# A token stage rearranged: zero fill of the slot buffers in eight parts, VectorE's order in the blocks, slot assignment, and a gather ring for the last group

## The chip, the cores and the metric

One core of one Trainium2 chip runs the whole kernel. The metric is the device time of one execution in microseconds (us). Inputs and outputs live in HBM; the core's five engines are TensorE (PE, with its weight loads shown apart as PEld), VectorE (DVE), ScalarE (ACT), GpSimd (POOL) and SyncE (SP). SP does no arithmetic here: it issues nearly all direct DMAs, in a hand-written order.

## What is computed

Two sequences of L = 2048 tokens with D = 256 features in float32. First an attention block is added to x, then a mixture of experts, run in two rounds (C = 2), is added to that:

```python
x = x + attention(layernorm(x))                # 16 heads of 64, causal, latent of 64
h = layernorm(x); xf = h
for j in range(2):                             # two rounds
    gate = xf @ router_W[j] + router_b[j]
    ids = top_2(gate + gate_bias[j])           # of E = 6 experts
    weights = softmax over the two of gate
    combined = sum of weights * expert(xf)     # up 256x256, silu gate 256x256, down
    share_out = two shared experts (xf)        # for every token
    y = xf + combined + share_out
    xf = y * rsqrt(mean(y*y) + EPS) * norm_w[j]
x = x + xf
```

To come near float32 accuracy a product is made of a high part and a low part of each operand, so most matrix products take three passes. A high part is written by ScalarE, its low part is the difference that VectorE or GpSimd takes.

## The kernel before, in words

build_weights (L69) and build_attention (L210) fill the first 1945 us; nothing in them is changed. build_tokens (L900) is the rest. It works on **blocks** of 512 tokens, 4 tiles of 128 each (TPB = 4). A sequence has 4 blocks (QB = 4), so a round has 8: r = 0 to 7 is round 0, r = 8 to 15 is round 1. A **group** g is a sequence in a round (g = 0 to 3), with 16 tiles of 128 tokens (JT = 16). A **unit** u = 4r + j is a tile of 128 tokens of block r in a round.

For a block of round 0 the kernel loads the attention's partial result (load_y, L971, four copies of 512 KB, i = 0 to 3), splits it (split_y on ScalarE, y_lo_even on VectorE), projects it (project on PE, L1161), adds the residual x (residual), takes mean and variance (moments, then rstd on GpSimd) and writes the normalized tokens into xcur (layernorm). Then, for blocks of both rounds: turn transposes them; the router gives 6 logits per token (L1194); choose (L1775) finds the top two and their weights; the shared expert goes up, gated and down in four k steps (L1228; gated, L1870, multiplies the silu by the up half on VectorE, and its result starts the next pair of matmuls), add_gated sums the halves, xt_lo and g_lo make low parts, take_shared(r) (L1886) adds the shared result to the tokens of block r one block later, and SP stores it (store_acc) to a buffer in HBM, from which load_acc fetches it later.

The two experts of a token are reached through **slots**. A group's 4096 (token, expert) pairs are sorted by expert into TILES = 37 tiles of 128 rows, SLOTS = 4736 rows of 1 KB. places and slots (L1844 to L1868) work out the row of each pair in the block that ends the group (r % 8 == 3 before the change), tile_experts which expert a tile has. GpSimd scatters the tokens to x_slots with indirect DMAs (L1629), 32 per group. Rows without a pair must be zero, so both x_slots buffers are filled from a zero tile before (L1081 to L1084); the first scatter waits for this through the semaphore "cleared". Behind the 8 blocks come tiles(c), 74 **expert tiles** with a load (load_tile, L1017), three layers and a store into e_slots. In the next round GpSimd gathers each token's two rows from e_slots (gather, L1640, into a ring of 4 buffers), and VectorE adds them with their weights (add_first and add_second, L1955 and L1962), takes variance; GpSimd makes the root (rms), VectorE normalizes. For units 16 to 31 (blocks 4 to 7) this lies in blocks 9 to 12: group 1's second half of round 0 is turned into the inputs of blocks 12 to 15 there. Units 48 to 63 (blocks 12 to 15, group 3) are done in a **tail** behind tiles(1), and so are the shared experts of blocks 14 and 15 (LATE).

Orders written out by hand: SP's queue (L1059 to L1147), and block_of of each engine: PE L1299, ACT L1490, POOL L1650, DVE L1987. An engine works strictly in its order. In VectorE's block_of before the change, a block of round 1 opened with eight adds of gathered rows and variance(r-5), then choose(r); a block of round 0 with moments(r+1) and choose(r), then layernorm(r+1) and two y_lo_even, and gated(r, 0) only behind these. In r = 3 and r = 11 places, slots and tile_experts closed the block. At the very end SP clears every semaphore of the stage one by one (clear_semaphores, L61), 99 of them.

## Time and profile before

| | us |
|---|---|
| median of 3 runs (lowest to highest) | 3025.83 (3025.55 to 3028.52) |
| the profiled execution: own time | 3039.41 |
| the profiled execution: span in the profile | 3037.7 |
| PE busy in the span | 2717.7 (89%) |
| DVE busy | 1923.0 (63%) |
| POOL busy | 1946.6 (64%) |
| ACT busy | 1721.3 (57%) |

The profile is of one execution; its own time is 13.6 us above the median of the runs. Times in a row are us from the start of the span unless marked ns. L12 is line 12 of the kernel before. A row of the timeline reads: start, duration, engine, line, operation, output<-inputs, shape, count of instructions put together, and in brackets how long the engine stood before it and for what. Tiles bear the name of the memory they lie in: the zero tile appears as accr, the ring of gathered rows and the raw y loads as yg, a loaded expert tile as work.

### The profile page before, as it was taken

What the parts mean: (1) busy time and instruction counts of PE and PEld (TensorE: products, weight loads), DVE (VectorE), ACT (ScalarE), POOL (GpSimd) and SP (SyncE); (2) the same over time, 40 slices, a digit from 0 to 9 for tenths busy, and PEclk for the clock granted to TensorE, in tenths of its full rate; (3) what the DMA queues carried; (4) which work ended last, traced back from release to release, by engine and by line L of the source; (5) the groups of instructions that cost most, each with busy time, mean ns of one, the idle gap of its engine ahead of it and who ended that gap; (6) DMA issues with size and microseconds to landing.
All of it is one profiled execution on the core that took longest, in us unless ns stands there. A gap on an engine that the chain in (4) does not pass through costs nothing. (4 is left out here: it accounts for less than half of the span.)

```text
span 3037.7 us, 57326 instructions
## 1 busy us (share of the span) xinstructions
PE 2717.7 (89%) x13656; PEld 2252.5 (74%) x13656; DVE 1923.0 (63%) x4379; ACT 1721.3 (57%) x4016; POOL 1946.6 (64%) x1743
## 2 busy tenths in 40 slices
PE   5899999999998599999999999689889997579993
PEld 4688778878886378787778788578777886468872
DVE  3777777777783677777777776245544463544555
ACT  2477777777777277777777778433223452214442
POOL 2588889888897289888898888522342232343234
PEclk9799999999999699999999999889989998779996
DMA  3001001000011101110010001373333441124452
GB/s 67 10 23 28 22 21 25 22 21 23 19 26 23 37 17 22 23 25 19 25 25 22 19 22 22 92 251 118 111 111 125 141 140 57 54 90 141 154 178 91
DMA packets 165661, 186.93 MB, mean 62 GB/s; under 512 B 56957, under 2 KB 130947, under 8 KB 165385
## 3 DMA queue, kind: packets, MB, share of 16 engines
q1 hardware_dynamic: 152072, 150.17, 16.8%
q0 software_dynamic: 12288, 33.57, 3.4%
q14 instruction: 196, 1.60, 0.3%
q8 instruction: 81, 1.33, 0.2%
q10 hardware_dynamic: 1024, 0.26, 0.0%
HBM read 100.56 MB, written 78.64 MB: 59 GB/s over the span
## 5 line engine op out<-in xcount | busy, mean ns | idle before, releaser
L363 POOL TENSOR_TENSOR pl<-pr,ph 128x512 fp32r<-128x512 f32 (+3 forms) x1184 | 1375.3, 1186 | 199.5 <-ACT ph L612 171.4
L609 ACT ACTIVATE pr<-ps 128x512 f32<-128x512 f32 (+3 forms) x1280 | 692.1, 541 | 430.4 <-DVE ps L737 192.0
L786 DVE TENSOR_REDUCE part<-ps 128x1 f32<-128x512 f32 (+3 forms) x1152 | 705.6, 618 | 142.8 <-PE ps L446 123.0
L612 ACT ACTIVATE ph<-ps 128x512 fp32r<-128x512 f32 (+3 forms) x1280 | 692.1, 541 | 0.0
L446 PE MATMUL ps<-k_hi,q_parts 128*128 128x512 f32 (+3 forms) x1280 | 496.2, 390 | 48.2 <-DVE part L786 23.5
L460 PE MATMUL ps<-q_parts,k_hi 128*128 128x512 f32 (+3 forms) x1280 | 488.1, 381 | 0.3
L480 PE MATMUL ps<-ph,v_hi 128*128 128x512 f32 (+3 forms) x1280 | 476.8, 372 | 8.1 <-POOL pl L363 8.0
L461 PE MATMUL ps<-q_row,k_lo 65*128 65x512 f32 (+3 forms) x1280 | 474.2, 370 | 0.0
L481 PE MATMUL ps<-ph,v_lo 128*128 128x512 f32 (+3 forms) x1280 | 470.0, 367 | 0.0
L482 PE MATMUL ps<-pl,v_hi 128*128 128x512 f32 (+3 forms) x1280 | 467.3, 365 | 0.0
L446 PEld LDWEIGHTS ps<-k_hi,q_parts 128*128 128x128 f32 x1280 | 247.7, 194 | 135.5 <-DVE part L786 59.2
L1228 PE MATMUL ps<-xt,share_up 128*128 128x512 f32 x768 | 228.2, 460 | 74.3 <-DVE work L1879 67.3
L480 PEld LDWEIGHTS ps<-ph,v_hi 128*128 128x128 f32 x1280 | 244.9, 191 | 62.9 <-POOL pl L363 17.3
L460 PEld LDWEIGHTS ps<-q_parts,k_hi 128*128 128x128 f32 x1280 | 243.8, 190 | 60.7 <-ACT ph L612 10.8
L481 PEld LDWEIGHTS ps<-ph,v_lo 128*128 128x128 f32 x1280 | 245.0, 191 | 38.1
L482 PEld LDWEIGHTS ps<-pl,v_hi 128*128 128x128 f32 x1280 | 242.8, 190 | 39.6
L461 PEld LDWEIGHTS ps<-q_row,k_lo 65*128 65x128 f32 x1280 | 244.7, 191 | 32.1
L1228 PEld LDWEIGHTS ps<-xt,share_up 128*128 128x128 f32 x768 | 169.6, 226 | 120.9 <-DVE work L1879 72.1
L737 DVE TENSOR_TENSOR ps<-ps,mask_kq 128x128 f32<-128x128 f32 x512 | 149.9, 293 | 154.2 <-PE ps L461 121.7
L1640 POOL DMA_INDIRECT yg<-e_slots,slot_i x128 | 125.1, 977 | 176.0 <-PE ps L1349 106.8
L1349 PE MATMUL ps<-exp_up,yy 128*128 x888 | 234.8, 400 | 0.0
L675 POOL TENSOR_TENSOR q_parts<-q_raw,q_parts 64x512 fp32r<-64x512 f32 x128 | 175.0, 1367 | 79.5 <-DVE q_parts L731 61.9
(203 smaller groups left out, 3830.1 us busy)
## 6 DMA issues: line engine op xcount, KB each, us to landing
work<-x_slots SPq DMA_DIRECT2D x148, 128.0 KB
e_slots<-work SPq DMA_DIRECT2D x148, 128.0 KB
rec<-recip_rows SPq DMA_DIRECT2D x128, 128.0 KB, 3.4
y_latent<-y_sums SPq DMA_DIRECT2D x128, 128.0 KB, 2.9
yg<-y_latent SPq DMA_DIRECT2D x32, 512.0 KB
x_slots<-accr SPq DMA_DIRECT2D x2, 4736.0 KB, 23.7
acc_shared<-accw SPq DMA_DIRECT2D x14, 512.0 KB
accr<-acc_shared SPq DMA_DIRECT2D x14, 512.0 KB
```

The lines of the kernel that those rows point to most:

```text
L363: eng.tensor_tensor(pl[:, s % RING, 0:w], pr[:, s % RING, 0:w], f32(ph[:, s % RING, 0:w]), ALU.subtract).then_inc(sem, 1)
L446: pe.matmul(ps[:, MAX_BANK + m % 2, 0:w], qa[half][:, i * P:(i + 1) * P], kh[:, c * BLK:c * BLK + w], start=True, stop=True).then_inc(S["m ...
L460: pe.matmul(out, kh[:, k], qa[half][:, q], start=True, stop=False)
L461: pe.matmul(out, kl[0:LD + 1, k], qc[half][:, q], start=False, stop=True).then_inc(S["scored"], 1)
L480: pe.matmul(out, va[:, kt, :], ph[:, b, 0:w], start=kt == 0, stop=False)
L481: pe.matmul(out, vc[:, kt, :], ph[:, b, 0:w], start=False, stop=False)
L482: pe.matmul(out, va[:, kt, :], pl[:, b, 0:w], start=False, stop=kt == TPB * (qb + 1) - 1).then_inc(S["latent_used"], 1)
L609: act.activation(pr[:, s % RING, 0:w], src, ACT.Exp).then_inc(S["probs"], 1)
L612: act.activation(ph[:, s % RING, 0:w], src, ACT.Exp).then_inc(S["probs_hi"], 1)
L786: ins = dve.tensor_reduce(dst, src[:, 0:w], AX.X, ALU.max)
L1228: mm = pe.matmul(out, sup[:, a, kind, n, dt, m * P:(m + 1) * P], xt[:, x, dt, :], start=i == 0, stop=i == len(terms) - 1)
L1349: mm = pe.matmul(out, tx[:, t % 2, x, dt, :], wu[:, b, bass.ds(expert[t], 1), dt, :], start=False, stop=n == len(terms) - 1)
```

## The change

- **Zero fill.** Instead of two copies of 4736 rows each ahead of the blocks, SP issues one part of 1184 rows (1.16 MB) in each of blocks 0 to 7, behind the block's loads and ahead of store_acc(r-1): 74 partitions write 16 rows of 1 KB each. Parts 0 to 3 fill buffer 0 (semaphore cleared0), 4 to 7 buffer 1 (cleared1); the first scatter of group 0 and of group 1 each wait for their own.
- **Start-up.** y loads 2 and 3 of block 0 are issued right behind x of block 0, ahead of the weights. ScalarE splits the router's weights behind all of split_y(0), VectorE its low part behind layernorm(0); PE makes the shared weights (make_shared) before turn(0, 0).
- **VectorE's order in a block.** choose, gated 0, weigh, gated 1, layernorm(r+1), normalize(r-6), (in r % 8 == 4) places and slots of the group before, y_lo_even, gated 2 and 3, xt_lo, take_shared, add_gated, then tile_experts, the adds of gathered rows and variance, the rest of y_lo_even, and moments(r+2) last. split_down is halved over blocks 6 and 7. ScalarE's squares follow its block work, and rms and normalize of a block of group 1 come one block later than before (10 <= r < 14).
- **Tail.** Group 3's gathers go to 16 buffers of their own (late, in the memory of the experts' up weights wu), each with its own semaphore, so they wait for no add. The low parts g_lo of blocks 14 and 15 move from GpSimd to VectorE (late_lo). The order of adds, take_shared(14) and normalize is rearranged, and two silus of block 15 go ahead of four squares.
- Semaphores of the stage: 17 more (cleared becomes two, 16 late).

Indentation is shortened in the diff:

```diff
...
   with ExitStack() as ctx:
-    names = ["small_in", "stage0", "stage1", "filled", "zeroed", "cleared",
+    names = ["small_in", "stage0", "stage1", "filled", "zeroed", "cleared0", "cleared1",
...
          "gathered0", "gathered1", "gathered2", "gathered3",
+         *[f"late{n}" for n in range(JT)],
...
     eo = wk[:, 8 * D:12 * D].rearrange("p (k d) -> p k d", d=D)
+    late = f32(W["wu"][:, :, :, :, :]).rearrange("p a e t i -> p (a e t i)")[:, 0:2 * JT * D].rearrange("p (u k d) -> p u k d", k=2, d=D)
...
-        load_y(0, 0)
-        load_y(0, 1)
+        for i in range(2):
+          load_y(0, i)
         load_x(0)
+        for i in range(2, 4):
+          load_y(0, i)
...
                  w["router_w"][c].rearrange("(t p) e -> p t e", p=P)).then_inc(S["small_in"], DMA)
-        load_y(0, 2)
-        load_y(0, 3)
...
         load_y(2, 1)
-        sp.wait_ge(S["zeroed"], 1)
-        for b in range(2):
-          sp.dma_start(x_slots[b].rearrange("(t p) d -> p t d", p=P),
-                 F["zero"][:, None, :].broadcast_to([P, TILES, D])).then_inc(S["cleared"], DMA)
...
             load_expert(2 * r + 3)
+          if r == 0:
+            sp.wait_ge(S["zeroed"], 1)
+          sp.dma_start(x_slots[r // QB].rearrange("(a p k) d -> a p k d", a=QB, k=16)[r % QB],
+                 F["zero"][0:SLOTS // 64, None, :].broadcast_to([SLOTS // 64, 16, D])).then_inc(S[f"cleared{r // QB}"], DMA)
...
         project(0)
+        make_shared()
         turn(0, 0)
-        make_shared()
...
-        def split_down():
+        def split_down(es):
           act.wait_ge(S["proj"], PAIRS * 8)
-          for e in range(E):
+          for e in es:
...
             bias_hi()
-          if r == 6:
-            split_down()
+          if r in (6, 7):
+            split_down(range(3 * (r - 6), 3 * (r - 5)))
...
           split_y(0, pair)
+        for pair in range(4, PAIRS):
+          split_y(0, pair)
...
         act.activation(W["router"][:, 0], F["router_raw"][:, :, :, :], ACT.Copy).then_inc(S["router_hi"], 1)
-        for pair in range(4, PAIRS):
-          split_y(0, pair)
...
         for r in blocks(1):
+          block_of(r)
...
               square(u)
-          block_of(r)
...
         g_hi(14)
+        silu(15, 0)
+        silu(15, 1)
...
           square(u)
-        silu(15, 0)
-        silu(15, 1)
...
             pool.wait_ge(S["slots"], g + 1)
-          if g == 0 and n == 0:
-            pool.wait_ge(S["cleared"], 2 * DMA)
+          if n == 0 and g < 2:
+            pool.wait_ge(S[f"cleared{g}"], 4 * DMA)
...
               pool.wait_ge(S[f"eo_stored{k}"], DMA * len([t for t in range(TILES * (g + 1)) if t % 4 == k]))
-          if u >= 4:
+          if 4 <= u < 3 * JT:
...
           for k in ks:
-            pool.indirect_dma_start(out=gath[:, u % 4, k, :], out_offset=None, in_=e_slots[g % 2],
+            out, sem = (late[:, j, k, :], S[f"late{j}"]) if g == 3 else (gath[:, u % 4, k, :], S[f"gathered{u % 4}"])
+            pool.indirect_dma_start(out=out, out_offset=None, in_=e_slots[g % 2],
                         in_offset=bass.IndirectOffsetOnAxis(F["slot_i"][:, g % 2, k, j:j + 1], axis=0)
-                        ).then_inc(S[f"gathered{u % 4}"], DMA)
+                        ).then_inc(sem, DMA)
...
         def block_of(r):
-          if 9 <= r < 13:
-            rms(r - 5)
+          if 10 <= r < 14:
+            rms(r - 6)
...
         tiles(1)
-        for u in range(48, 52):
-          gather(u)
-        g_lo(14)
-        for u in range(52, 54):
+        for u in range(48, 58):
...
         rms(12)
-        for u in range(54, 58):
+        for u in range(58, 62):
...
         rms(13)
-        for u in range(58, 60):
-          gather(u)
-        g_lo(15)
-        for u in range(60, 64):
+        for u in range(62, 64):
...
-        def split_down():
-          for e in range(E):
+        def split_down(es):
+          for e in es:
...
           row = accr[:, u // 4 % 2, u % 4, :]
-          late = u // TPB in LATE
-          if late and u % 4 == 0:
+          last = u // TPB in LATE
+          if last and u % 4 == 0:
...
             dve.wait_ge(S[f"acc_in{u // 4 % 2}"], DMA * (u // 8 + 1))
-          base = xcur[:, 1, j // TPB, j % TPB, :] if late else row
-          dve.wait_ge(S[f"gathered{u % 4}"], 2 * DMA * (u // 4 + 1))
-          dve.scalar_tensor_tensor(out=row, in0=gath[:, u % 4, 0, :], scalar=F["mix"][:, g % 2, 0, j:j + 1], in1=base,
+          base = xcur[:, 1, j // TPB, j % TPB, :] if last else row
+          if g == 3:
+            dve.wait_ge(S[f"late{j}"], 2 * DMA)
+          else:
+            dve.wait_ge(S[f"gathered{u % 4}"], 2 * DMA * (u // 4 + 1))
+          got = late[:, j, 0, :] if g == 3 else gath[:, u % 4, 0, :]
+          dve.scalar_tensor_tensor(out=row, in0=got, scalar=F["mix"][:, g % 2, 0, j:j + 1], in1=base,
...
           dve.wait_ge(S["add_a"], u + 1)
-          dve.scalar_tensor_tensor(out=row, in0=gath[:, u % 4, 1, :], scalar=F["mix"][:, g % 2, 1, j:j + 1], in1=row,
+          got = late[:, j, 1, :] if g == 3 else gath[:, u % 4, 1, :]
+          dve.scalar_tensor_tensor(out=row, in0=got, scalar=F["mix"][:, g % 2, 1, j:j + 1], in1=row,
...
         def block_of(r):
-          if 9 <= r < 13:
-            for u in range(16 + 4 * (r - 9), 20 + 4 * (r - 9)):
-              add_first(u)
-              add_second(u)
-            variance(r - 5)
-          if r + 1 < 8:
-            moments(r + 1)
           choose(r)
+          if r not in LATE:
+            gated(r, 0)
+          weigh(r)
+          if r not in LATE:
+            gated(r, 1)
...
             layernorm(r + 1)
+          if 10 <= r < 14:
+            normalize(r - 6)
+          if r % 8 == QB:
+            places(r // QB - 1)
+            slots(r // QB - 1)
...
           if r not in LATE:
-            gated(r, 0)
-          weigh(r)
-          if 9 <= r < 13:
-            normalize(r - 5)
-          if r not in LATE:
-            for k in range(1, 4):
-              gated(r, k)
+            gated(r, 2)
+            gated(r, 3)
...
               add_gated(r, m)
+          if r % 8 == QB:
+            tile_experts(r // QB - 1)
+          if 9 <= r < 13:
+            for u in range(16 + 4 * (r - 9), 20 + 4 * (r - 9)):
+              add_first(u)
+              add_second(u)
+            variance(r - 5)
...
             first_tiles(r // QB)
-            places(r // QB)
-            slots(r // QB)
-            tile_experts(r // QB)
-          if r == 6:
-            split_down()
+          if r in (6, 7):
+            split_down(range(3 * (r - 6), 3 * (r - 5)))
+          if r + 2 < 8:
+            moments(r + 2)
...
           y_lo_even(0, pair)
-        dve.wait_ge(S["router_hi"], 1)
-        dve.tensor_tensor(W["router"][:, 1], F["router_raw"][:, :, :, :], f32(W["router"][:, 0]),
-                  ALU.subtract).then_inc(S["router_lo"], 1)
...
         layernorm(0)
+        dve.wait_ge(S["router_hi"], 1)
+        dve.tensor_tensor(W["router"][:, 1], F["router_raw"][:, :, :, :], f32(W["router"][:, 0]),
+                  ALU.subtract).then_inc(S["router_lo"], 1)
...
         residual(1)
+        moments(1)
...
         tiles(1)
+        def late_lo(r):
+          for m in range(2):
+            dve.wait_ge(S["g_hi"], 2 * r + m + 1)
+            dve.tensor_tensor(gg[:, 1, m, :], g0[:, m, :], f32(gg[:, 0, m, :]), ALU.subtract).then_inc(S["g_lo"], 1)
+
+        def units(us):
+          for u in us:
+            add_first(u)
+            add_second(u)
+
...
           add_gated(14, m)
-        for u in range(48, 52):
-          add_first(u)
-          add_second(u)
+        late_lo(14)
+        units(range(48, 52))
...
         variance(12)
+        units(range(52, 54))
...
           add_gated(15, m)
-        for u in range(52, 56):
-          add_first(u)
-          add_second(u)
+        late_lo(15)
+        units(range(54, 56))
...
         variance(13)
-        for u in range(56, 58):
-          add_first(u)
-          add_second(u)
+        units(range(56, 60))
+        take_shared(14)
         normalize(13)
-        for u in range(58, 60):
-          add_first(u)
-          add_second(u)
-        take_shared(14)
         variance(14)
-        for u in range(60, 64):
-          add_first(u)
-          add_second(u)
+        units(range(60, 64))
```

## Rows read from the trace of the kernel before

**Rows 1.** Windows: length, busy us (instructions) per engine, PE clock, DMA share, GB/s

```profile
1945.00:2047.00 102.00, 76.26 (x458) 68.82 (x459) 42.48 (x100) 28.53 (x49) 27.50 (x64) 0.82 0.72 243
...
2512.00:2721.00 209.00, 145.29 (x696) 124.25 (x696) 99.10 (x265) 40.95 (x93) 81.59 (x80) 0.76 0.20 69
2721.00:2950.00 229.00, 222.25 (x1334) 193.65 (x1335) 115.99 (x307) 103.16 (x328) 65.44 (x68) 0.98 0.46 145
2950.00:3037.70 87.70, 36.61 (x160) 30.09 (x158) 47.13 (x95) 17.96 (x48) 42.64 (x40) 0.69 0.35 116
```

**Rows 2.** PE's waits: total us, times, mean; 2047 to 2277, then 2512 to 2710

```profile
PE ps L1228 <- DVE work L1879: 22.4, 6, 7.2
...
PE ps L1228 <- DVE work L1879: 43.8, 4, 12.2
```

**Rows 3.** Timeline around the fill and block 2's projection

```profile
1991.39 12.19 SPq L1083 DMA_DIRECT2D x_slots<-accr  x2
...
2028.44 7.45 PE L1161 MATMUL ps<-nn,yy 128*128 128x256 f32 x48 [10.60 <-DVE yy L1738]
```

**Rows 4.** Timeline, start-up and block 0

```profile
1956.57 0.95 SPq L977 DMA_DIRECT2D yg<-y_latent  x2
...
1962.66 7.43 PE L1161 MATMUL ps<-nn,yy 128*128 128x256 f32 x48 [3.09 <-DVE yy L1738]
...
1994.34 2.74 PE L1194 MATMUL ps<-router,xt 128*128 128x6 f32 x24
...
2041.39 2.84 PE L1194 MATMUL ps<-router,xt 128*128 128x6 f32 x24
```

**Rows 5.** Timeline, block 2 and the first load of an expert tile

```profile
2079.57 2.84 PE L1194 MATMUL ps<-router,xt 128*128 128x6 f32 x24
...
2100.22 1.28 DVE L1900 TENSOR_TENSOR accw<-ps,xcur 128x512 f32<-128x512 f32 x2
...
2103.27 1.14 ACT L1428 ACTIVATE yy<-yg 128x512 fp32r<-128x512 f32 x2
...
2279.27 1.32 SPq L1027 DMA_DIRECT2D work<-x_slots  x3
```

**Rows 6.** A DMA queue; issues (KB each, us to landing); a window of the fill

```profile
q10 hardware_dynamic: 1024, 0.26, 0.0%
...
x_slots<-accr SPq DMA_DIRECT2D x2, 4736.0 KB, 23.7
...
q_row<-max_rows ACTq DMA_DIRECT2D x128, 2.0 KB
...
2006.00:2010.00 4.00, 4.00 (x23) 3.35 (x22) 0.93 (x2) 0.69 (x1) 0.00 (x0) 1.00 1.09 386
```

**Rows 7.** Timeline, blocks 10 to 15

```profile
2577.90 0.48 DVE L1955 SCALAR_TENSOR_TENSOR accr<-yg,mix,accr 128x256 f32<-128x256 f32 x1 [6.95 <-DMA yg<-e_slots,slot_i]
...
2590.67 5.04 PE L1228 MATMUL ps<-xt,share_up 128*128 128x512 f32 x12 [11.89 <-DVE work L1879]
...
2603.20 1.28 DVE L1884 TENSOR_TENSOR work<-work 128x512 f32<-128x512 f32 x2
...
2624.33 5.26 PE L1228 MATMUL ps<-xt,share_up 128*128 128x512 f32 x12 [12.04 <-DVE work L1879]
...
2690.29 0.69 ACT L1445 ACTIVATE work<-ps,share_b_gate 128x512 f32<-128x512 f32 x1 [6.41 <-remote]
```

**Rows 8.** Timeline of the tail; last instructions of the stages, by queue

```profile
2998.48 0.48 DVE L1955 SCALAR_TENSOR_TENSOR accr<-yg,mix,xcur 128x256 f32<-128x256 f32 x1 [3.12 <-DMA out<-accr]
...
3001.91 4.38 DVE L1985 TENSOR_TENSOR accr<-accr,x1t 128x256 f32<-128x256 f32 x4
...
3025.01 1.42 DVE L1985 TENSOR_TENSOR accr<-accr,x1t 128x256 f32<-128x256 f32 x4
...
L65 ACTq DRAIN  x4: 14/14/14, 35.4 to 3031.6; - x4
...
L65 SPq DRAIN  x4: 7/7/7, 35.9 to 3037.5; - x4
```

## What the change was predicted to do, before it was run

> **What bounds the kernel now.** I read the stretches by stage first [rows 1]: attention ends at 1945 us and is untouched. Behind it come a start-up and token blocks 0 to 7 (to 2277), the expert tiles of round 0 (2277 to 2512), blocks 8 to 15 (to 2721), the tiles of round 1 (to 2950) and a tail. In the tiles of round 1 PE is busy for 222.25 of 229 us at a clock of 0.98 (round 0 is alike); in blocks 8 to 15 it is busy for 145.3 of 209 us at 0.76, in the tail for 36.6 of 87.7. So the tiles are PE's, and everything that the change can reach lies between them. The waits [rows 2] say what PE waits for: gated(r, 0) on VectorE, 22.4 us in blocks 1 to 7 and 43.8 us in four blocks of the second round. The timeline [rows 3] shows the zero fill: two copies of 4736 KB each [rows 6] hold SP's queue for 12.19 us from 1991.4, block 2's y loads stand behind them, and PE stands for 10.6 us in front of block 2's projection.
>
> **Start-up, the loads moved forward.** y loads 2 and 3 of block 0 are issued at 1956.57 [rows 4], behind 14 copies; PE waits 3.1 us and projects until 1970.1. In front of the weights they can go out some 3.5 us earlier, as soon as GpSimd has freed the buffers, so project(0) ends near 1965.5. The weights and small copies go out 7.5 us later; the last lands near 1967, when make_shared (5.6 us and 1 us) now fits ahead of turn(0). project(1) and the block move up with it: block 0 starts near 1987.5 (1994.34 now [rows 4]): gain 7. Block 0 lasts 47.05 us from that row to the next block's [rows 4]; without the 10.6 us, the 1.1 in front of gated and the slow projection it lasts 34. Block 1 then starts at 2021, 20 us earlier.
>
> **VectorE's order, blocks 1 to 7.** gated(r, 0) stood behind layernorm and two y_lo_even (1.4 and 1.3 us); in block 4 also behind places, slots and tile_experts (about 3.5), in block 7 behind six splits, which wait for down weights. [...] moments keeps its place in time. layernorm now follows gated(r, 1) and ends about when turn needs it; split_down's second half costs 2 us before the tiles, under the first tile's load. By PE alone the tiles would start 46 us earlier.
>
> **The fill in eight parts** is the unknown. The two copies together are 9472 rows of 1 KB; 386 GB/s over 16 engines [rows 6] makes that 592 rows on each engine, 25.1 us. A part has 1184 rows from 74 partitions. How many engines take it, no row shows. The nearest rows: ScalarE's q_row copies have 4 rows, and their queue holds 1024 packets for 128 of them, 8 each, so 4 data packets and 4 completions: one engine per row, not 16 [rows 6]. Copies of 128 rows use all 16, 8 rows each. Both are equal shares of the outermost dimension. 74 has equal whole shares on 2 engines (37 each) or on 1; unequal ones would use 16. The bounds of a part are then 74 rows per engine, 3.1 us, and 592 rows, 25.1 us on two engines (23 at the 4096-byte packets' rate of 159 ns, 27.2 at the 46 ns a 1 KB packet shows). I take the second: it continues what both kinds of copy do. [...]
>
> On two engines every part holds back each later copy of SP's queue, since each has a share there. Walked through with PE's steps: part 1 runs 2026 to 2051. Block 1's y loads, due 23.7 us into a block (2079.57 to 2103.27 [rows 5]), so at 2045, land at 2053.4; block 2 starts at 2068 with a slow projection. Part 2 (2073 to 2098) keeps store_acc(0), which take_shared(1) needs 20.65 us into block 2 (2100.22 [rows 5]), 11.4 us late. Block 3 starts at 2118; part 3 runs 2113 to 2138, part 4 2152 to 2177, and from then on the queue hardly runs dry: parts 5 to 7 until 2221, 2256 and 2287 with the scatters' packets between them. Six loads of down weights stand behind part 7, and choose(7) behind them on VectorE. Part 8, issued ahead of load_tile, runs 2293.5 to 2318.6; the first tile lands at 2322, now about 2281.5 (issue 2279.27 [rows 5], 2.2 us). As a tally: 201 us of fill, 56 for 21.5 MB of other copies, 10.6 for 32 scatters of 128 KB, 28 dry, from 2026: 2322. **Loss 40 instead of a gain of 46.** The store to the slots is not needed sooner: the scatters wait until 2178 for part 4, which costs GpSimd's low halves 6.5 us in block 4 (counted). Tiles of round 0: 0.
>
> **Blocks 8 to 15.** Now choose(r) waits for eight adds that wait for gathers issued a block earlier, only just in front of them: 6.95 us for the first [rows 7], and PE stands 11.9 us. New, the adds come last, by which time the rows have landed. One block, from one k=2 start to the next: to the end of add_gated 13.8 (2590.67 to 2604.48 [rows 7]), eight adds at 0.48 make 3.8, g_lo on GpSimd collides with them (four adds of a residual row take 4.38 beside one, 1.42 without [rows 8]) for 1.95, square and variance 0.7, choose 3.1, gated 0.75: 24.1 instead of 33.66. [...] rms(r-6) stands behind eight gathers of 1.26 us on GpSimd; normalize ends 0.7 us before gated(r, 2) could go anyway. The 32 scatters start 17 us earlier than now and end near 2682. Tiles of round 1 start near 2685.5 against 2721 [rows 1]; two waits of 3.4 us on something unrecorded, one in [rows 7], may recur, so **gain 32**, ends 24 and 36.
>
> **Tail.** 32 gathers no longer wait for buffers, and g_lo moves to VectorE (1.35 us each, no collision). But rms(12) stops GpSimd for 3.6 us since its squares now follow two silus, and unit 56 still waits for out of block 12 to be written (3.12 us [rows 8]) at 2998.3, as now. From there units 56 to 59, take_shared, normalize(13), the same 3.1 us of writing, units 60 to 63, normalize(14) and (15): end at 3022 against 3026.4: gain 4.5. SP clears 17 more semaphores; 99 take 5.9 us [rows 8], so 1 more.
>
> **Sum**: +40 - 32 - 4.5 + 1 = +4.5 us against the profiled execution, span 3037.7, own time 3039.41; that is 13.6 above the median of the three runs, 3025.83, to which I carry the difference: **3030.3**. 0.2% is 6 us, about what a measurement of this kernel can tell from no change.
>
> **Rivals.**
> (a) The parts spread over 16 engines. For: a 1 KB row needs 42 ns there, and nothing in the trace forbids unequal shares; against: the 4-row copies. Then -46 - 32 - 3.5 = -81.5: 2944. Chance 0.12.
> (b) Slower: GpSimd's and the queue's delays add up. The mechanism is a part's length on two engines: at the 46 ns of a packet 27.2 us, and what the parts delay is chained from part 1 to load_tile, so 8 x 2.1 = +17; blocks 8 to 15 unchanged: 3047. It decides when a part is above about 25.8 us (3036, 0.2% over). For: nothing overlaps packets on a lone engine; against: 42.4 ns each in the fill now. Chance 0.28.
> (c) Faster on two engines: HBM or the fabric limits the 16, and a lone engine runs at 4096-byte speed: 23 us a part, -17: 3013. Chance 0.13.
> (d) Only half of the 32 us come, because rms(r-6) behind late gathers becomes the wait in front of gated(r, 2) and turn(r+1): +16, 3046. Against: 0.7 us to spare, rows landed a block before. Chance 0.12.
> The forecast has the rest, 0.35.
>
> **Numbers.** Range 3000 to 3060: it holds the forecast and (b) to (d) with the ends 24 and 36 and 5 us for the start-up; (a) is left out with its 0.12. Faster by over 0.2%: (a), (c) and a tenth of the forecast's spread, 0.31. Within: 0.27. Slower: (b), (d) and a little, 0.42.
>
> **What would show it.** Right: long stretches of blocks 1 to 7 with DMA share near 0.12 and each later SP copy landing up to 25 us late; PE waiting for take_shared's store in block 2 and some 30 us for gated(7, 0); load_tile landing near 2322; k=2 starts 24 us apart in blocks 10 to 12; unit 56 still waiting for out. Wrong: a part that lands within 6 us of its issue with 386 GB/s shows (a). An interval of 33 us in blocks 10 to 12 would show another wait in the place of the gathers.

## The result, and the profile after

| | before | after |
|---|---|---|
| median of 20 runs, us | 3026.39 (3020.37 to 3033.62) | 3032.85 (3027.63 to 3040.17) |
| ratio after / before | | 1.0020, interval 1.0013 to 1.0027 |
| profiled execution: own time / span, us | 3039.41 / 3037.7 | 3034.35 / 3032.4 |

The kernel became 0.2% slower, 6.5 us between the medians; the forecast was +4.5 us and 3030.3 us. The two profiled executions by themselves say the opposite, -5.1 us, since that of before lay 13.0 us above its median and that of after 1.5 us. What sets them apart is told under the experiments.

The windows of after, cut at its own stage ends (start:end, length, busy us and count of PE, PEld, DVE, ACT, POOL, PE clock, DMA share, GB/s); [rows 1] answer to them:

```profile
1945.00:2322.00 377.00, 275.03 (x1680) 242.52 (x1680) 174.19 (x408) 90.98 (x161) 109.31 (x130) 0.86 0.41 137
2322.00:2558.00 236.00, 226.35 (x1364) 199.61 (x1364) 115.73 (x301) 104.18 (x330) 65.51 (x68) 0.97 0.42 131
2558.00:2724.00 166.00, 141.73 (x688) 120.78 (x688) 101.09 (x259) 39.63 (x90) 83.42 (x80) 0.81 0.23 80
2724.00:2940.00 216.00, 211.34 (x1285) 186.08 (x1286) 110.93 (x295) 98.75 (x316) 64.81 (x67) 0.99 0.49 153
2940.00:3032.40 92.40, 44.66 (x208) 36.84 (x207) 49.34 (x111) 21.88 (x61) 37.62 (x37) 0.74 0.35 116
```

Start-up and blocks 0 to 7 now reach to 2322 instead of 2281, with PE busy for 275 of 377 us. Blocks 8 to 15 take 166 us instead of 205. The two cancel. SP's timeline (columns as ahead of the prediction) shows the first. L1101 issues a part of the fill, L994 is store_acc, L979 a y load, L1029 the load of expert tiles:

```profile
2023.73 0.80 SPq L1101 DMA_DIRECT2D x_slots<-accr  x1
2032.79 14.15 SPq L979 DMA_DIRECT2D yg<-y_latent  x2
...
2071.16 0.68 SPq L1101 DMA_DIRECT2D x_slots<-accr  x1
2071.89 22.62 SPq L994 DMA_DIRECT2D acc_shared<-accw  x1
...
2226.85 27.62 SPq L994 DMA_DIRECT2D acc_shared<-accw  x1
...
2284.39 9.50 SPq L1017 DMA_DIRECT2D yg<-in_exp_down  x6
2293.93 0.68 SPq L1101 DMA_DIRECT2D x_slots<-accr  x1
2309.31 6.73 SPq L994 DMA_DIRECT2D acc_shared<-accw  x1
2316.15 2.49 SPq L1029 DMA_DIRECT2D work<-x_slots  x3
```

A part itself is issued in 0.7 us. Behind each of the first seven parts the next large copy then needs 14 to 28 us to be issued; behind the eighth, whose next copy comes 15 us later, 6.7 us. In variant 32 below store_acc takes 1.7 us right behind a part and 0.3 us some time after it. So the queue is held while a part drains. A window behind the fourth part shows how little moves meanwhile, a DMA share of 0.14, where the prediction named 0.12 as its sign:

```profile
2155.00:2175.00 20.00, 17.23 (x86) 14.30 (x86) 16.30 (x55) 4.97 (x9) 3.62 (x3) 0.91 0.14 49
```

The engines wait for what stands behind; PE's and GpSimd's timeline at four places:

```profile
2054.28 8.45 PE L1163 MATMUL ps<-nn,yy 128*128 128x256 f32 x48 [9.42 <-DVE yy L1735]
...
2105.65 4.69 PE L1163 MATMUL ps<-nn,yy 128*128 128x256 f32 x19 [13.36 <-DVE yy L1735]
...
2181.40 1.24 POOL L1631 DMA_INDIRECT x_slots<-xcur,slot_i  x1 [18.07 <-DMA x_slots<-accr]
...
2297.83 7.89 PE L1230 MATMUL ps<-xt,share_up 128*128 128x512 f32 x24 [32.21 <-DVE work L1876]
...
2322.79 1.34 PE L1335 MATMUL ps<-ident,work 128*128 128x128 f32 x4 [13.81 <-DMA work<-x_slots]
```

The row at 2297.83 is gated(7, 0) behind choose(7), behind splits of down weights that were loaded only when part 7 had let the queue go (VectorE stands 28.4 us in front of one of these splits). The last row is the first expert tile, whose load stands behind part 8; before it started at 2281.5.

In blocks 8 to 15 the waits of [rows 7], 11.9 and 12.0 us, are down to 3.8, 2.2 and 3.4 us, and the starts lie 24.5 and 25.1 us apart instead of 33.7:

```profile
2613.98 0.79 PE L1230 MATMUL ps<-xt,share_up 128*128 128x512 f32 x1 [3.77 <-DVE work L1876]
...
2638.44 0.73 PE L1230 MATMUL ps<-xt,share_up 128*128 128x512 f32 x2 [2.21 <-DVE work L1876]
...
2663.58 0.78 PE L1230 MATMUL ps<-xt,share_up 128*128 128x512 f32 x2 [3.42 <-DVE work L1876]
```

In the tail unit 56 still waits for out to be written, 2.13 us (3.12 in [rows 8]); the last adds come at 3018.79 (3025.01), and SP clears its semaphores in 6.7 us, from 3025.4 to 3032.1 (5.9):

```profile
2997.79 0.48 DVE L1956 SCALAR_TENSOR_TENSOR accr<-exp_up,mix,xcur 128x256 f32<-128x256 f32 x1 [2.13 <-DMA out<-accr]
...
3018.79 1.42 DVE L1987 TENSOR_TENSOR accr<-accr,x1t 128x256 f32<-128x256 f32 x4
...
L65 ACTq DRAIN  x4: 14/14/14, 35.4 to 3025.4; - x4
...
L65 SPq DRAIN  x4: 7/7/7, 35.9 to 3032.1; - x4
```

### The profile page after: what moved, and what is told of

Read it like the earlier page. It is cut to its first block and busy times, and to the rows that moved or that the text cites. A ratio compares the mean times of both kernels' runs of the same rounds, so it can differ in the third digit from the quotient of the medians.

```text
span 3032.4 us, 57352 instructions
## 1 busy us (share of the span) xinstructions
PE 2701.1 (89%) x13656; PEld 2244.8 (74%) x13656; DVE 1930.6 (64%) x4383; ACT 1719.7 (57%) x4016; POOL 1940.6 (64%) x1739
## 5 line engine op out<-in xcount | busy, mean ns | idle before, releaser
L1230 PE MATMUL ps<-xt,share_up 128*128 128x512 f32 x768 | 217.3, 443 | 56.6 <-DVE work L1876 51.5
L1631 POOL DMA_INDIRECT x_slots<-xcur,slot_i x128 | 125.3, 979 | 184.1 <-PE ps L1351 82.5
L1230 PEld LDWEIGHTS ps<-xt,share_up 128*128 128x128 f32 x768 | 161.3, 215 | 100.0 <-DVE work L1876 55.8
```

Source lines behind the costliest of these rows:

```text
L1230: mm = pe.matmul(out, sup[:, a, kind, n, dt, m * P:(m + 1) * P], xt[:, x, dt, :], start=i == 0, stop=i == len(terms) - 1)
```

## The experiments

The kernels were run in four batches (jobs), each together with runs of the kernel before, and each ratio is to those runs. The jobs were not alike: the median of before was 3023.3 us beside e1 to e4, 3042.8 beside e5 to e8 on the same chip, 3041.5 beside e9 and e10, 3039.0 beside e11 and e12. So times in us are compared within a job, and between jobs ratios, which is rougher: what made a job slower need not cost every kernel the same. "Variant 32" is the changed kernel with parts of 32 partitions; it was run as such in the first job only. The diffs are shortened: tile and semaphore names stand without their dictionaries, and ... stands for the rest of a line.

| kernel | ratio to before, interval | start-up | blocks 0-7 | blocks 8-15 | tail |
|---|---|---|---|---|---|
| before (profile ahead of the prediction) | 1 | 43.2 | 287.1 | 205.4 | 92.7 |
| after | 1.0020 (1.0013 to 1.0027) | 36.3 | 337.3 | 166.5 | 85.8 |
| e1_rows32 (variant 32) | 0.9752 (0.9733 to 0.9772) | 36.4 | 249.6 | 164.3 | 87.0 |
| e2_before_parts74 | 1.0197 (1.0175 to 1.0219) | 44.5 | 343.6 | 200.4 | 92.8 |
| e3_before_parts32 | 0.9980 (0.9966 to 0.9994) | 40.4 | 272.8 | 200.1 | 92.9 |
| e4_old_fill | 0.9787 (0.9769 to 0.9805) | 36.2 | 269.7 | 164.3 | 86.8 |
| e6_act_queue | 0.9824 (0.9804 to 0.9843) | 36.1 | 270.9 | 170.1 | 100.5 |
| e7_adds_first | 0.9921 (0.9898 to 0.9944) | 35.9 | 260.2 | 210.7 | 100.3 |
| e8_old_tail | 0.9759 (0.9736 to 0.9781) | 37.2 | 253.5 | 167.8 | 94.1 |
| e9_old_start | 0.9806 (0.9788 to 0.9824) | 42.8 | 260.0 | 170.1 | 100.6 |
| e10_down_early | 0.9779 (0.9756 to 0.9802) | 36.1 | 253.5 | 166.0 | 100.6 |
| e11_rows128 | 0.9753 (0.9735 to 0.9772) | 38.9 | 255.2 | 163.9 | 98.9 |
| e12_rows128_old_tail | 0.9754 (0.9733 to 0.9774) | 37.3 | 255.7 | 166.8 | 92.9 |

The stages are differences of start times of PE's instructions in each kernel's trace: first projection to the router of block 0; to the first expert tile; router of block 8 to the first tile of round 1; last tile to the last drain of the engines other than SP. The first projection itself lay anywhere from 1946 to 1956 us, in code that no kernel changed. Equal code also gives unequal stages: blocks 0 to 7 are the same in e7 and e8 and took 260.2 and 253.5 us in one job, and the old start-up took 40.4 to 44.5 us in before, e2, e3 and e9. So differences of up to about 7 us between two profiles are not read as effects here. e5, a measurement of copies, is left out of the table.

**Shape of the parts, in the changed kernel (e1_rows32).**

```diff
-x_slots[r // QB].rearrange("(a p k) d -> a p k d", a=QB, k=16)[r % QB], zero[0:74, None, :].broadcast_to([74, 16, D])
+x_slots[r // QB].rearrange("(a p k) d -> a p k d", a=QB, k=37)[r % QB], zero[0:32, None, :].broadcast_to([32, 37, D])
```

> The changed kernel, with each part of the fill written as 32 partitions of 37 rows instead of 74 partitions of 16 rows: same bytes, same place in SP's queue. Theory (a part of 74 partitions runs on two of the 16 DMA engines, 25 us each, and holds the queue; 32 partitions go over all 16, 3 to 4 us each): the first expert tile starts near 2235 to 2245 us instead of 2322.8, and the time is 2935 to 2960, 2.2 to 3% under before. Rival 1 (the fill is limited by HBM writes or by the position in the queue whatever its shape): 3025 to 3035, no change from the changed kernel. Rival 2 (the engines' bound behind the fill is higher than I walked): the copies land early, but the time only falls to 2975 to 3000.

Measured: 0.9752, 2950.75 us beside 3023.31, 2.5% faster than before. The same bytes at the same place in the queue cost 87.7 us less in blocks 0 to 7 (337.3 to 249.6); no copy of SP's queue but two groups of six loads takes over 4 us to issue. Rival 1 is out, and so is rival 2. A part with the store_acc behind it, and the first tile's row:

```profile
2065.49 0.58 SPq L1101 DMA_DIRECT2D x_slots<-accr  x1
2066.12 1.67 SPq L994 DMA_DIRECT2D acc_shared<-accw  x1
...
2242.20 0.44 PE L1335 MATMUL ps<-ident,work 128*128 128x128 f32 x2 [3.77 <-DMA work<-x_slots]
```

**The fill alone, in the kernel before (e2, e3), and the old fill in the changed one (e4).** The edit of e2 is the fill's hunks of the change alone; e3 has them with the shape of e1; e4 takes the parts out and has the old copies, each with its own semaphore:

```diff
 load_y(2, 1)
+sp.wait_ge(S["zeroed"], 1)
+for b in range(2):
+    sp.dma_start(x_slots[b].rearrange("(t p) d -> p t d", p=P), zero[:, None, :].broadcast_to([P, TILES, D])) ...
 load_expert(0)
...
-sp.dma_start(x_slots[r // QB] ...)
```

> The kernel before with the eight-part fill of 74 partitions alone, everything else as it was. Theory (the parts chain up in SP's queue and fill about 290 us whatever VectorE does): first expert tile near 2325 to 2340, blocks 8 to 15 and tail as before, so 3065 to 3085, 1.3 to 2% slower than before. Rival (the parts only hurt because the rearranged blocks run faster than the queue): under 3045.

> The kernel before with the eight-part fill as 32 partitions of 37 rows, everything else as it was. Theory: the 10.6 us stall in front of block 2's projection and the 12 us of blocked queue go, each part takes 3 to 4 us beside other work: 3010 to 3018, 0.3 to 0.5% faster than before. Rival (parts disturb loads in each block): same time or slower, 3026 and up.

> The changed kernel with the fill as before (two copies of 4736 rows ahead of the blocks), everything else changed. Theory (start-up 7, VectorE's order in blocks 1 to 7 some 25, blocks 8 to 15 37, tail 7 us of gain are independent of the fill; the fill's stall of some 11 us stays): 2950 to 2965, 2 to 2.5% faster. Rival (the gains of the blocks need the early y loads that only the parts allow): 2975 to 2990.

Measured: 1.0197 (3083.65 us), 0.9980 (3017.27) and 0.9787 (2962.26). The times lie within the theories' numbers; as a ratio e3 is 0.2% faster and falls short of the 0.3 to 0.5% expected. With parts of 74 partitions the kernel before waits as the changed one does, at the same two places:

```profile
2079.16 22.59 SPq L992 DMA_DIRECT2D acc_shared<-accw  x1
...
2313.11 8.46 PE L1228 MATMUL ps<-xt,share_up 128*128 128x512 f32 x24 [34.93 <-DVE work L1879]
```

So the parts of 74 set the length of blocks 0 to 7 almost alone: 343.6 us with the old order, 337.3 with the new. Of the 23 us that the changed order and start-up give there with good parts (272.8 to 249.6) all but 6 are swallowed. Splitting the fill is itself worth little: 6 us in e3, and from e4 to e1 11.5 us.

**What sets the time of a part (e5_shapes).**

```diff
+sp.wait_ge(S["zeroed"], 1)
+for n, (a, k) in enumerate([(74,16),(37,32),(32,37),(16,74),(8,148),(100,12),(127,9),(128,9),(120,10)]):
+    sp.dma_start(x_slots[0][0:a * k, :].rearrange("(p k) d -> p k d", k=k), zero[0:a, None, :].broadcast_to([a, k, D])) ...
+    sp.wait_ge(S["probe"], DMA * (n + 1))
```

> A measurement in the variant with parts of 32 partitions: ahead of all other work of the token stage SP issues nine zero copies of about 1150 to 1200 rows of 1 KB one after the other, each waited for: partitions x rows 74x16, 37x32, 32x37, 16x74, 8x148, 100x12, 127x9, 128x9, 120x10. Theory (equal whole shares of the partitions on the largest number of engines up to 16 that divides them, 42 to 46 ns a row, and about 2 us of latency): on 2, 1, 16, 16, 8, 10, 1, 16 and 15 engines, so 27, 52, 5, 5, 8.5, 7, 50, 5 and 5.5 us. Rival (a long copy is spread in some other way, and 74 was slow because of its 16 KB runs in DRAM): 37x32 as slow as 74x16 or faster, 127x9 near 5 us. The time of the kernel is that of the variant and about 160 us.

SP's timeline; each copy starts when the one before it has landed:

```profile
1950.86 0.86 SPq L1063 DMA_DIRECT2D x_slots<-accr  x1
...
1978.05 0.71 SPq L1063 DMA_DIRECT2D x_slots<-accr  x1
...
2029.97 0.62 SPq L1063 DMA_DIRECT2D x_slots<-accr  x1
...
2037.64 0.57 SPq L1063 DMA_DIRECT2D x_slots<-accr  x1
...
2051.17 0.73 SPq L1063 DMA_DIRECT2D x_slots<-accr  x1
...
2076.60 0.88 SPq L1063 DMA_DIRECT2D x_slots<-accr  x1
...
2085.88 0.69 SPq L1063 DMA_DIRECT2D x_slots<-accr  x1
...
2136.29 0.58 SPq L1063 DMA_DIRECT2D x_slots<-accr  x1
...
2141.10 0.90 SPq L1063 DMA_DIRECT2D x_slots<-accr  x1
...
2148.91 0.82 SPq L979 DMA_DIRECT2D yg<-y_latent  x2
```

The differences are 27.2 us for 74x16, 51.9 for 37x32, 7.7 for 32x37, 13.5 for 16x74, 25.4 for 8x148, 9.3 for 100x12, 50.4 for 127x9, 4.8 for 128x9 and 7.8 for 120x10. Windows inside the first, second and fifth copies show the engines at work, DMA share and GB/s last:

```profile
1952.00:1976.00 24.00, 0.00 (x0) 0.00 (x0) 0.00 (x0) 0.00 (x0) 2.35 (x41) 0.50 0.13 47
1980.00:2028.00 48.00, 0.00 (x0) 0.00 (x0) 0.00 (x0) 0.00 (x0) 0.00 (x0) 0.50 0.07 24
...
2053.00:2075.00 22.00, 0.00 (x0) 0.00 (x0) 0.00 (x0) 0.00 (x0) 0.00 (x0) 0.50 0.41 51
```

A share of 0.13 is two of 16 engines, 0.07 one, 0.41 near eight that are not busy throughout. The rival is out: it wanted 37x32 no slower than 74x16 and 127x9 near 5 us. The copies of 74, 37 and 127 partitions behave as the largest divisor up to 16 asks: 2, 1 and 1 engines, at 24 GB/s each (47, 24 and, from 2088 to 2134, 24 GB/s); 127 partitions took ten times as long as 128. The packets of all nine say the same: besides those of 1 KB, a copy has 2, 1, 16, 16, 8, 10, 1, 16 and 15 packets under 512 B, in the order above, which for each is the number of engines that the theory names. The copies of 16 and 8 partitions fell outside the expectation by 8.5 and 17 us, those of 32, 100 and 120 by 2.3 to 2.7: the number of engines is not the only bound (below). With them the nine copies took 198 us instead of the 160 or so expected.

**Where the part is queued (e6_act_queue).** The part of 74 partitions is issued by ScalarE, and SP issues none:

```diff
 def block_of(r):          # ScalarE
+    if r < 8:
+        act.dma_start(x_slots[r // QB] ..., zero[0:74, None, :].broadcast_to([74, 16, D])) ...
     if r + 2 < 8:
```

> The changed kernel with its 74-partition parts issued by ScalarE at the head of its block work instead of by SP. The parts still take 25 us on two engines, but nothing stands behind them in their queue. Theory (the loss is mostly the order of SP's queue; on the two engines the loads share with the parts): 2955 to 2985. Rival (the two engines themselves are the limit, whatever the queue): over 3010.

Measured: 0.9824, 2988.81 us beside 3042.80; the time is 4 us above the expected range, the gain of 54 us within what it meant beside 3026. Blocks 0 to 7 took 270.9 us. Against the changed kernel 66 of the 88 us are back, though the parts are no faster: the packets of one part in ScalarE's own queue spread over 29 to 41 us. Against the 253.5 to 260.2 us of e7, e8 and e10, 11 to 17 are still lost. So most of the harm is what stood behind the part in its queue; the rest is told apart no further. ScalarE's own issue of a part took 7 to 15 us in blocks 4 to 7, loads may still meet the parts on the two engines, and the parts also go out at another point of a block than in the changed kernel.

**VectorE's order in round 1 (e7_adds_first).** In variant 32 the adds, variance, rms(r-5) and the squares of blocks 9 to 12 are back where the kernel before has them, and normalize(r-5) is back in its block, behind layernorm:

```diff
 def block_of(r):
+    if 9 <= r < 13:
+        for u in range(16 + 4 * (r - 9), 20 + 4 * (r - 9)): add_first(u); add_second(u)
+        variance(r - 5)
     choose(r)
...
-        normalize(r - 6)
+        normalize(r - 5)
```

> The variant with parts of 32 partitions, with VectorE's adds, variance and normalize of blocks 9 to 12, GpSimd's rms and ScalarE's squares put back as in the kernel before (adds in front of choose). Theory (choose waits for adds that wait for gathers issued just before): k=2 starts 33 us apart again in blocks 10 to 12, blocks 8 to 15 longer by 30 to 39 us: 2981 to 2990. Rival (part of the gain in blocks 8 to 15 comes from gated ahead of layernorm and weigh alone): 2965 to 2975.

Measured: 0.9921 against 0.9752, 51 us of 3026, and 52 us more than e8 in the same job; blocks 8 to 15 take 210.7 us, 41 to 47 more than in the other variants. The mechanism stands, PE waits 12.03 us again in front of k=2:

```profile
2590.64 1.65 PE L1230 MATMUL ps<-xt,share_up 128*128 128x512 f32 x3 [12.03 <-DVE work L1876]
```

Its size was missed: 30 to 39 us were expected. 210.7 us is also 5 to 11 us more than the kernel before itself takes there (200.1 to 205.4); the rest of the new order, places and slots in block 12 among it, stays in e7, but no run shows that this is the reason.

**Start-up, down weights and tail (e9, e10, e8).** e9 puts y loads 2 and 3, make_shared and the router's split back as before, e8 the whole tail; e10 issues parts 4 to 7 in blocks 4 and 5 and four load_down ahead of store_acc(5). All start from variant 32:

```diff
-load_x(0); load_y(0, 2); load_y(0, 3); up_t ...        # e9, SP
+load_x(0); up_t ...; load_y(0, 2); load_y(0, 3)
-make_shared(); turn(0, 0)                              # e9, PE
+turn(0, 0); make_shared()
...
+if r == 6: load_down(0) to load_down(3)                # e10, SP
 if r: store_acc(r - 1)
...
-for u in range(48, 58): gather(u)                      # e8, GpSimd
+for u in range(48, 52): gather(u)
+g_lo(14)
```

> The variant with parts of 32 partitions, with the start-up of the kernel before (y loads 2 and 3 of block 0 behind the weights, make_shared behind turn, the router's split in front). Theory (first projection to block 0 takes 43.2 us before and 36.4 in the variant): 6 to 8 us slower than the variant, 2956 to 2959. Rival (block 1's loads are the next wait, so most of it is made up by block 1): 2951 to 2953.

> The variant with parts of 32 partitions, with two parts each in blocks 4 and 5 and none in 6 and 7, and the first four down weights loaded ahead of store_acc(5). Theory (PE waits 3.8 us for gated(7, 0) because choose(7) stands behind splits of down weights that wait for store_acc(5) in SP's queue): 2 to 4 us faster than the variant, 2946 to 2949. Rival (the first tile's load waits for g_sum of block 7 anyway, and the splits only move): no change, 2950 to 2952.

> The variant with parts of 32 partitions, with the tail of the kernel before: ring of 4 buffers for group 3, g_lo of blocks 14 and 15 on GpSimd, the old order. Theory (the tail gains 6 us in the profiles, start of the tail to the last add, 1 given back by 16 semaphores that are now gone as well): 2955 to 2958. Rival (the ring only moves a wait, as out of block 12 is waited for in both): 2950 to 2952.

Measured: e9 0.9806, e10 0.9779, e8 0.9759. e9 and e10 ran side by side: the old start-up costs 6.7 us in the profiles' start-up (42.8 against 36.1) and 7.4 us between the medians (2983.65 and 2976.30), as its theory said, if e10 stands for variant 32. The profiles' blocks 0 to 7 differ by another 6.5 us (260.0 and 253.5), no more than e7 and e8 do with equal code, so this is not put down to the start-up. In e10 PE's wait of 3.8 us for gated(7, 0) is down to 1.2 at most, but the first tile waits 3.8 us for its load, as in e1 (3.77): the rival's mechanism. In time e10 shows no gain over variant 32 (0.9779 against 0.9752, intervals overlap), but variant 32 was not run beside it, so 2 us are not excluded. e8 equals variant 32 within the intervals, against the 6 us that its theory expected; since its job was another, the tail was tried again.

**All 128 partitions, with both tails (e11, e12).**

```diff
+x_slots[r // QB].rearrange("(p t) d -> p t d", p=P)[:, 9 * (r % QB):9 * (r % QB) + (9 if r % QB < 3 else 10), :]
```

> The changed kernel with each part of the fill written by all 128 partitions, 9 rows each (10 in every fourth part), instead of 74 partitions of 16 rows. In the shapes run 128x9 took 4.8 us and 32x37 took 7.7, since one partition gave no more than 1 KB per 160 ns. Theory (both shapes are hidden beside other work, so only the 16 engines matter): ratio to before 0.973 to 0.977, the same as with 32 partitions (0.9752); first tile 285 to 287 us after the first projection. Rival (the shorter parts also free the y loads behind them): 0.970 to 0.973, first tile 3 us or more earlier.

> The same kernel with the tail of the kernel before: ring of 4 buffers, g_lo of blocks 14 and 15 on GpSimd, the old order, 16 semaphores fewer. Theory (the new tail is shorter by about 6 us in the profiles): 5 to 7 us slower than the kernel with 128 partitions, on the same chip. Rival (in the last job each of three variants with the new tail showed a 16 us stall of PE at its start that falls in no releaser, and the old tail none; if that stall belongs to the new tail, it costs more than the ring gives): 5 to 10 us faster.

Measured in one job: 2964.97 us (0.9753) and 2966.98 us (0.9754). The ratio of e11 is that of 32 partitions, as the theory had it. Its first tile came 294 us after the first projection and not at 285 to 287; e8 and e10 have 290.7 and 289.6 there, e1 286.0. For e12 neither theory nor rival holds: 2 us slower, not clear of noise. The new tail gives nothing in this job, and its stage is 6 us longer here (98.9 against 92.9), where in the first job's traces it is 6 us shorter (87.0 and 86.8 against 92.8 and 92.9). ScalarE's timeline of e11 shows what came in between, with the last of GpSimd's first 20 gathers (L1643):

```profile
2877.40 0.69 ACT L1447 ACTIVATE work<-ps,share_b_gate 128x512 f32<-128x512 f32 x1 [7.12 <-issue]
...
2886.76 0.69 ACT L1447 ACTIVATE work<-ps,share_b_gate 128x512 f32<-128x512 f32 x1 [5.72 <-remote]
...
2894.38 0.95 POOL L1643 DMA_INDIRECT exp_up<-e_slots,slot_i  x1 [0.30 <-issue]
...
2898.76 0.69 ACT L1447 ACTIVATE work<-ps,share_b_gate 128x512 f32<-128x512 f32 x1 [11.30 <-remote]
```

ScalarE waits for nothing of the program at 2887.5 to 2898.8, and goes on 4.4 us after the last of 20 gathers in a row was issued. In the five other traces with the new tail from these jobs (e5, e6, e7, e9, e10) the same wait ends 4.5 to 4.7 us after that gather; in e8 and e12, whose gathers wait for a ring of four, there is none. But after, e1 and e4 have the same 20 gathers in a row and no such wait, so the gathers alone don't make it. What ScalarE waits for isn't shown, and no run took it away by itself: its cause stays open.

Such waits also set the two profiles of the result apart. ScalarE's waits put down to "issue" or "remote" in the token stage add up to 78 us in the trace of before and to none in that of after, nor in e1 to e4; all eight traces of the later jobs (e5 to e12) have them. The groups of before:

```profile
ACT junk L1547 <- issue: 29.8, 6, 8.9
ACT work L1445 <- remote: 20.9, 3, 12.8
ACT work L1524 <- issue: 12.4, 11, 1.1
```

They include the wait of 6.41 us in [rows 7]. So they look like a condition of the job and not of the kernel: within each job all traces agree, and the own time of before's profile, 3039.41 us, is that of before in the later jobs. It isn't proved, since no kernel was profiled in both kinds of job, and the waits say where time went and not that they are all of the 13 us. The fairer base for after's stages are e2 and e3: blocks 8 to 15 200.1 to 200.4 us instead of 205.4, tail 92.8 to 92.9.

## Why the prediction was right, step by step

**The fill** was the step that decided, and it held. A part of 1184 rows on two engines was forecast at 25.1 us and took 27.2 with its latency when it ran alone (e5); the first tile was forecast at 2322 and came at 2322.8, the first scatter at 2178 and came at 2181.4, PE's wait for gated(7, 0) at some 30 and was 32.2. The way there was less exact: take_shared(1) was to be 11.4 us late and VectorE waited 14.6 us for it in block 2. The forecast "loss 40 instead of a gain of 46" is 43.3 us (the sum of start-up and blocks 0 to 7: 330.3 to 373.6) against 44.3 us (286.0 in e1). Rival (a), the parts over 16 engines, was wrong for this kernel, and e1 shows what it would have given: forecast at -81.5 us and measured at 0.9752, -75. Rivals (b) and (c) were other lengths of a part: 27.2 us in (b) is what e5 shows for one landed part, but that has the latency in it, and two engines moved 47 GB/s, 1 KB per 43 ns each, so (b)'s 46 ns did not come: that is the median length of a 1 KB packet, in before's fill as in e5, but in e5's first copy 2.16 of them were under way at a time on the two engines. (c)'s 159 ns is the median packet of 4096 bytes in before, 1991 to 2030 us, and its 23 us did not come either. The step from the q_row copies holds: one of them (64 to 72 us of before) has 8 packets, 4 of them under 512 B, and two copies of 128 rows (82 to 90 us) have 288, 32 of them under 512 B, so 16 each; in e5 such packets are as many as the engines at work, 2 beside a DMA share of 0.13, 1 beside 0.07.

**Start-up**: forecast 7, measured 6.9 (43.2 to 36.3), and 7.4 us between the medians of e9 and e10. That the profiles hit the forecast so closely is chance: the old start-up took 40.4 to 44.5 us in four traces and the new one 35.9 to 38.9.

**VectorE's order, blocks 1 to 7**: some 25 of the forecast's 46 us, as e4's expectation names it. No run shows this term, since none changes VectorE's order in these blocks alone; in its place the runs showed 23.2 us for blocks 0 to 7 from e3 to e1, and 17.4 from before to e4, both with the old fill. Both pairs change the start-up too, so the size of this step stays open between the two. It could not be seen in the changed kernel itself.

**Blocks 8 to 15**: forecast 32 with ends 24 and 36. Against the profile before 38.9, against e2 and e3, 33.8. One block was forecast at 24.1 us and took 24.5 and 25.1. The start at 2685.5 asks for 35.5, of which the step from 33.66 to 24.1 gives 9.56 for each of blocks 10 and 11; no run shows the rest as the forecast's terms. Measured from router to router blocks 9 to 13 gain 11.0, 9.0, 12.1, 7.5 and -3.6, 36.0 in all, block 8 loses 1.5 and blocks 14 and 15 gain 4.4. A shorter wait in front of k=2 did not always give faster matmuls: 12 of them took 5.04 us at a granted clock of 0.56 behind 11.89 us in before (from 2590.67), 5.49 at 0.50 behind 3.77 in after (from 2613.98), and 3.06 at 1.00 behind 2.21 (from 2638.44). Here the step on the two waits of 3.4 us "that may recur" was the right doubt with the wrong reading: before has 3.44 us in front of the router of block 14 and 6.06 us near the end of block 15, where e3 and after have no wait at the first place and 2.6 us at the second. So they belonged to the execution that was profiled.

**Tail**: forecast 4.5, measured 6.9 against before and 7.0 against e2 and e3, where ScalarE's waits are absent; in jobs that have them, nothing. **Semaphores**: forecast 1, measured 0.8 (5.9 to 6.7).

**The sum** was close because the fill was sized rightly, and by luck beyond that. Measured on the two profiles the terms come to +43.3 - 38.9 - 6.9 + 0.8 = -1.7 us, and another 3.6 us of the spans' -5.3 lie in stages that no term speaks of (the first projection 2.0 earlier, the tiles of round 1 2.9 shorter, those of round 0 1.2 longer). Against a base without ScalarE's waits the terms are +43.3 for the way to the first tile (up to 3.8 more, since before took 21.8 us from the router of block 6 to that of block 7 and e3 18.0), -33.8, -7 and +0.8, so +3 to +7, where the medians show +6.5. Against the forecast's terms the way to the first tile is 3.3 us longer or more, blocks 8 to 15 are 1.8 and the tail 2.5 shorter: errors of the size of the result, which cancel. The step "13.6 above the median, to which I carry the difference" took the whole profile as evenly inflated; it was not. With terms of 40 and 32 us known to a few us each, the sign of a sum of 4.5 was not known beforehand; the prediction says so in its chances, 0.42 for slower, with 0.31 for faster, which by its own list, (a), (c) and a tenth of the forecast's 0.35, is 0.285.

## What to carry to other kernels

Before a DMA is cut into parts, look at the outermost count of each part: the same bytes took 27.2 us from 74 partitions and 7.7 from 32, with 88 us between them in blocks 0 to 7 of this kernel. A slow copy does most of its harm here through the copies behind it in its own queue (66 of 88 us), so gains elsewhere (17 of 23 us here) can vanish behind one, and undoing one edit at a time is what shows them. When an engine's waits in a profile name no releaser, compare several executions of the same kernel before a term is taken from them.

## What was not expected of the hardware

From few source partitions a copy was slower than its engines. Of 128x9's 4.8 us, 72 rows an engine at 42 ns (386 GB/s over 16 engines in [rows 6]) leave about 2 us of latency. The copy of 8x148 then took 148 rows at 158 ns from each partition, 16x74 74 rows at 156 ns and 32x37 37 rows at 154 ns; in the window of 8x148 51 GB/s moved, 6.4 GB/s for each partition, where one engine moved 24 GB/s from 37 partitions. So an estimate for a zero copy of this kind is about 2 us and the larger of 42 ns for each row of an engine and 157 ns for each row of a partition. Whether that second bound belongs to a partition or to something that neighbouring partitions share isn't shown: the sources were always partitions 0 to 7, 0 to 15 and 0 to 31. The zero source was one row per partition in all of them. And 100x12 and 120x10 took 2.3 us more than their 10 and 15 engines ask for by 42 ns a row; why is open.
